# Normalising each 512-query block of a head inside the attention loop instead of after it

## The reference

```
q, k = l2norm(q) * qs, l2norm(k) * ksc;  q, k = rotary_xpos(q, k)
sim  = einsum('bhwid,bhwjd->bhwij', q * 8, k)
mask = (i < j) | (i > j + 512) | (j == -1)
attn = softmax(where(mask, -big, sim))
o    = einsum('bhwij,bhwjd->bhwid', attn, v)
x    = x + o @ wo
```

## Time and profile before

| what | value |
|---|---|
| median of 11 runs | 3704.29 us (3684.22 to 3756.74) |
| time of the profiled execution | 3687.03 us |
| span of its slowest core (core 1) | 3685.5 us |
| busy share of the span, core 1 | PE 70%, PEld 26%, DVE 42%, ACT 15%, POOL 14% |

### The profile page before, as it was taken

How to read it: one execution, slowest core, us unless ns; L and a number is a source line. 1 busy time by engine, 2 the same in 40 slices (tenths; PEclk the granted TensorE clock), 3 DMA queues, 4 the chain that set the end, 5 groups by cost and what they waited for, 6 DMA issues and landing times.

```text
span 3685.5 us, 34257 instructions; the slowest of 8 cores (3657.7 to 3685.5 us)
## 1 busy us (share of the span) xinstructions
PE 2584.8 (70%) x10044; PEld 950.2 (26%) x10044; DVE 1536.2 (42%) x2354; ACT 563.7 (15%) x862; POOL 516.8 (14%) x933
## 2 busy tenths in 40 slices
PE   3636994666787864489999756677777438998970
PEld 2212331221121211034434322112121203343420
DVE  3863664564434334322321256544443422232216
ACT  0100121112121210211011011122212021001101
POOL 3000001000000003052343100000000124235210
PEclk9767997775555558599999877555555859999985
DMA  5022002000000003485575100000000166558522
GB/s 78 0 35 35 15 15 57 1 1 1 1 1 1 1 12 40 67 108 83 69 107 76 32 16 0 1 1 1 0 1 1 21 98 87 82 77 114 77 54 91
DMA packets 136866, 143.08 MB, mean 39 GB/s; under 512 B 33436, under 2 KB 115356, under 8 KB 136688
## 3 DMA queue, kind: packets, MB, share of 16 engines
q0 software_dynamic: 129632, 128.01, 24.0%
q1 hardware_dynamic: 7056, 12.88, 1.0%
HBM read 249.90 MB, written 12.58 MB: 71 GB/s over the span
## 4 chain that ended last, share of the span: by engine, by line
PE 52%; DVE 23%; issue 8%; DMA 7%; ACT 5%; POOL 3%; DVEq 1%; ACTq 0%; SPq 0%; POOLq 0%
PE pA L1074 6%; PE pG L1079 6%; PE pP L292 5%; PE pX3a L1130 5%; PE pX3b L1130 4%; PE pAV L724 4%; DMA W1g<-w_i 3%; DVE g2f L313 3%; DVE scr L679 3%; PE pST L744 2%; PE pST L741 2%; PE pWo L827 2%; PE pS L744 1%; PE pS L741 1%; PE pS L666 1%
## 5 line engine op out<-in xcount | busy, mean ns | idle before, releaser
L1074 PE MATMUL pA<-HN,W1a 128*128 128x512 bf16 (+1 forms) x1408 | 348.7, 392 | 76.2 <-DMA W1g<-w_i 45.2
L1098 DVE SCALAR_TENSOR_TENSOR HG<-pA,b1ac,scr 128x512 bf16<-128x512 f32 (+1 forms) x176 | 132.1, 750 | 553.2 <-ACT scr L1093 553.2
L1079 PE MATMUL pG<-HN,W1g 128*128 128x512 bf16 (+1 forms) x1408 | 341.1, 386 | 0.0
L1056 POOL DMA_DIRECT2D W1a<-w_i x352 | 214.4, 609 | 704.8 <-PE pG L1079 700.3
L1093 ACT ACTIVATE scr<-pG,b1gc 128x512 bf16<-128x512 f32 (+1 forms) x176 | 121.2, 689 | 829.9 <-PE pG L1079 829.9
L527 PE MATMUL pQKV<-AQ,XT 128*128 128x512 bf16 x768 | 228.2, 468 | 8.7 <-DVE rope L501 8.6
L764 DVE TENSOR_TENSOR APT<-APT,m 128x128 bf16<-128x128 bf16 x256 | 57.6, 225 | 418.5 <-ACT APT L760 418.5
L1060 POOL DMA_DIRECT2D W1g<-w_i x352 | 217.5, 618 | 17.2 <-issue 17.2
L810 POOL DMA_DIRECT2D AO<-wo_i x8 | 4.3, 557 | 1484.2 <-DVE AoT L793 1484.2
L1074 PEld LDWEIGHTS pA<-HN,W1a 128*128 128x128 bf16 (+1 forms) x1408 | 138.2, 100 | 258.2 <-issue 107.1
L292 PE MATMUL pP<-WqkvT,XT 128*128 128x512 bf16 x768 | 189.7, 392 | 0.0
(11 more groups left out here) (223 smaller groups left out, 3352.9 us busy)
## 6 DMA issues: line engine op xcount, KB each, us to landing
W1a<-w_i POOLq DMA_DIRECT2D x320, 128.0 KB, 6.4
W1g<-w_i POOLq DMA_DIRECT2D x320, 128.0 KB, 6.7
W2i<-w_i POOLq DMA_DIRECT2D x42, 256.0 KB, 26.6
wst<-Wqkv POOLq DMA_DIRECT2D x24, 256.0 KB, 4.3
AQ<-wqkv_i POOLq DMA_DIRECT2D x16, 384.0 KB, 14.1
XS<-x POOLq DMA_DIRECT2D x16, 256.0 KB, 16.2
x1h<-XS SPq DMA_DIRECT2D x16, 256.0 KB, 2.0
out<-of_sb SPq DMA_DIRECT2D x8, 512.0 KB, 3.1
```

The source lines that it names most:

```text
L1056: E("ge", lambda e, j=j, b5=b5, wa=wa, l=l, bb=bb: e.dma_start(out=W1a[bb][:, 512 * j:512 * j + wa], in_=self.dw1[l, 128 * j:128 * (j + 1) ...
L1074: ins = e.matmul(pA[pp][0:wh, :], W1a[bb][:, 512 * j + 128 * i5:512 * j + 128 * i5 + wh], HNc[:, 512 * j:512 * (j + 1)], start=(j == 0), s ...
L1079: ins = e.matmul(pG[pp][0:wh, :], W1g[bb][:, 512 * j + 128 * i5:512 * j + 128 * i5 + wh], HNc[:, 512 * j:512 * (j + 1)], start=(j == 0), s ...
L1098: E("ve", lambda e, wh=wh, pc=pcglob, pp=pp: e.scalar_tensor_tensor(HG[0:wh, 512 * pc:512 * (pc + 1)], pA[pp][0:wh, :], b1ac[0:wh, pc:pc + ...
```

## The change

The tail of a head is cut into four blocks of 512 queries, each in two halves. `emit_rblock_a(b)` puts the logarithm and the exponential of block b's 512 sums on ScalarE's queue and the copy of block b on VectorE's; `emit_rblock_b(b)` puts the spreading matmul on TensorE's queue and the multiply on VectorE's. For blocks 0, 1 and 2 they are called inside the loop of pass 2: the first half in iteration kc = 4b + 4 after the AV of chunk 4b + 3, the second half in iteration kc = 4b + 5 after the AV of chunk 4b + 4. Block 3 follows after the loop. The waits are on the AV that completes the block, on the block's own exponential and on the block's own matmul. No DMA is changed.

```diff
+            def emit_rblock_a(b):
+                pe_cl = pe_av_last[(h, min(4 * b + 3, NT - 1))]
+                E("se", lambda e, b=b: e.activation(
+                    rw5[0:1, 512 * b:512 * (b + 1)],
+                    pAV[64:65, 512 * b:512 * (b + 1)], AF.Ln),
+                  wait=[("pe", pe_cl)])
+                E("se", lambda e, b=b: e.activation(
+                    rwb[0:1, 512 * b:512 * (b + 1)],
+                    rw5[0:1, 512 * b:512 * (b + 1)], AF.Exp, scale=-1.0))
+                se_rb[b] = C["se"]
+                E("ve", lambda e, b=b, g=g, base=base: e.tensor_copy(
+                    AoT[base:base + 64, 2048 * g + 512 * b:2048 * g + 512 * (b + 1)],
+                    pAV[0:64, 512 * b:512 * (b + 1)]),
+                  wait=[("pe", pe_cl)])
+
+            def emit_rblock_b(b):
+                E("pe", lambda e, b=b: e.matmul(
+                    pAV[64:128, 512 * b:512 * (b + 1)], self.cones[0:1, 0:64],
+                    rwb[0:1, 512 * b:512 * (b + 1)], start=True, stop=True),
+                  wait=[("se", se_rb[b])], inc=[("pe", 1)])
+                pe_rbc[b] = C["pe"]
+                E("ve", lambda e, b=b, g=g, base=base: e.tensor_tensor(
...
+                    pAV[64:128, 512 * b:512 * (b + 1)], op=OP.mult),
+                  wait=[("pe", pe_rbc[b])])
...
                     emit_av(kc - 1, min(640, T - 128 * (kc - 1)))
+                    if (kc - 1) % 4 == 3:
+                        emit_rblock_a((kc - 1) // 4)
+                    if kc >= 5 and (kc - 5) % 4 == 0:
+                        emit_rblock_b((kc - 5) // 4)
             emit_av(NT - 1, min(640, T - 128 * (NT - 1)))
-            E("se", lambda e: e.activation(rw5[:], pAV[64:65, 0:2048], AF.Ln),
-              wait=[("pe", pe_av_done), ("pe", C["pe"])])
-            E("se", lambda e: e.activation(rwb[:], rw5[:], AF.Exp, scale=-1.0))
...
-            for qc in range(4):
-                E("ve", lambda e, qc=qc, g=g, base=base: e.tensor_copy(
...
-                  wait=[("pe", pe_av_done)])
-                E("pe", lambda e, qc=qc: e.matmul(
...
-                  wait=[("se", se_r)], inc=[("pe", 1)])
...
-                E("ve", lambda e, qc=qc, g=g, base=base: e.tensor_tensor(
...
-                  wait=[("pe", pe_rbc[qc])])
+            emit_rblock_a(3)
+            emit_rblock_b(3)
```

More of the change, by code:

```diff
@@ L731, in emit_av @@
                 pe_av_last[(h, kc)] = C["pe"]
+            se_rb = {}
+            pe_rbc = {}
+            def emit_rblock_a(b):
[19 more added lines that the diff above has]
+                E("ve", lambda e, b=b, g=g, base=base: e.tensor_tensor(
+                    AoT[base:base + 64, 2048 * g + 512 * b:2048 * g + 512 * (b + 1)],
+                    AoT[base:base + 64, 2048 * g + 512 * b:2048 * g + 512 * (b + 1)],
+                    pAV[64:128, 512 * b:512 * (b + 1)], op=OP.mult),
+                  wait=[("pe", pe_rbc[b])])
             for kc in range(NT):
@@ L774, in layer_att @@
                     emit_av(kc - 1, min(640, T - 128 * (kc - 1)))
+                    if (kc - 1) % 4 == 3:
+                        emit_rblock_a((kc - 1) // 4)
+                    if kc >= 5 and (kc - 5) % 4 == 0:
+                        emit_rblock_b((kc - 5) // 4)
             emit_av(NT - 1, min(640, T - 128 * (NT - 1)))
-            pe_av_done = C["pe"]
-            E("se", lambda e: e.activation(rw5[:], pAV[64:65, 0:2048], AF.Ln),
-              wait=[("pe", pe_av_done), ("pe", C["pe"])])
-            E("se", lambda e: e.activation(rwb[:], rw5[:], AF.Exp, scale=-1.0))
-            se_r = C["se"]
-            pe_rbc = {}
-            for qc in range(4):
-                E("ve", lambda e, qc=qc, g=g, base=base: e.tensor_copy(
-                    AoT[base:base + 64, 2048 * g + 512 * qc:2048 * g + 512 * (qc + 1)],
-                    pAV[0:64, 512 * qc:512 * (qc + 1)]),
-                  wait=[("pe", pe_av_done)])
-                E("pe", lambda e, qc=qc: e.matmul(
-                    pAV[64:128, 512 * qc:512 * (qc + 1)], self.cones[0:1, 0:64],
-                    rwb[0:1, 512 * qc:512 * (qc + 1)], start=True, stop=True),
-                  wait=[("se", se_r)], inc=[("pe", 1)])
-                pe_rbc[qc] = C["pe"]
-                E("ve", lambda e, qc=qc, g=g, base=base: e.tensor_tensor(
-                    AoT[base:base + 64, 2048 * g + 512 * qc:2048 * g + 512 * (qc + 1)],
-                    AoT[base:base + 64, 2048 * g + 512 * qc:2048 * g + 512 * (qc + 1)],
-                    pAV[64:128, 512 * qc:512 * (qc + 1)], op=OP.mult),
-                  wait=[("pe", pe_rbc[qc])])
+            emit_rblock_a(3)
+            emit_rblock_b(3)
             ve_oT[h] = C["ve"]
```

## The result

The changed kernel takes 3612.71 us (median of 13 runs, 3588.95 to 3713.48), the kernel before 3697.87 (median of 48 runs, 3681.24 to 3816.07). The ratio is 0.9752, interval 0.9722 to 0.9781, which leaves out executions in which the cores of one die ran at a lower granted clock than the others. Of 3697.87 us that is 91.7 us, with about 11 to either side; 88.5 were forecast.

A forecast was written before the change was run, and what follows sets the result against it. TensorE sets the pace in pass 2 and waits for the tail after it. 7.29 - 0.96 - 0.80 = 5.53 us a head, 88.5 for 16 heads, takes the median from 3704.3 to 3616 us; range 3594 to 3636.

The forecast's parts named there:

- The tail: Behind the loop only block 3 stays: 3.03 us to the next head's reduction instead of 10.32, saving 7.29 a head.
- Blocks 0 and 1: In the loop of pass 2, each adds its spreading matmul's time to TensorE: 2 x 0.48 = 0.96 us a head.
- The wait: Spreading matmul of blocks 0 and 1, behind AV: reciprocals come in time, with 0.32 us to spare.
- The size of the matmul: Spreading matmul in the loop: 0.48 us of TensorE's time, between 0.45 and 0.54.
- Block 2: On short chunks 12 and 13: TensorE stalls 0.3 us, then runs 0.48; costs 0.80 a head, bounds 0.45 and 1.3.
- VectorE's and ScalarE's work at nothing: Blocks 0 and 1 in the loop: these engines' work costs nothing, covered by TensorE's own work.
- Stalls in the loop: Rival: each in-loop block makes TensorE wait for its reciprocals; only 20 us gained, 3684 us; chance 7 in 100.
- Table reloads: Rival: ScalarE loads its function table twice per block, 1.283 us each; 66 us slower, 3770; chance 3 in 100.
- A higher clock: Rival: TensorE granted 2.4 instead of 1.2 GHz in pass 2; 200 us more gained, about 3415; chance 2 in 100.
- the lower end of the gain: Whole kernel: bounds of block 2 and of the matmul give a gain of 80 to 95 us, 3609 to 3624.

The follow-up runs named there:

- e7: The changed kernel with all four blocks cut but kept behind the loop, every block waiting for the last AV; a head's period 59.78 us.
- e4_double_ln: The changed kernel with ScalarE's logarithm of blocks 0, 1 and 2 done twice in a row; a head's period 58.86 us against 57.46.
- e5_double_spread: The changed kernel with TensorE's spreading matmul of blocks 0, 1 and 2 done twice in a row; a head's period 58.77 us against 57.46.

## Why the prediction was right, and where its terms were off

**Where the gain comes from.** The forecast was 88.5 us from heads that are 5.53 us shorter; they are 5.56 shorter, and the span lost 90.1. The experiments split the 5.56 step by step:

| step | period, us | saves, us |
|---|---|---|
| before | 63.02 | |
| cut into four blocks, copies ahead of the multiplies, all waiting for the last AV (e7) | 59.78 | 3.24 |
| each block waits for its own AV (e1) | 58.91 | 0.87 |
| blocks 0 to 2 in the loop, second half one chunk later (the change) | 57.46 | 1.45 |
| the same without the one chunk (e2) | 62.59 | -3.68 against e1 |

My theory (A in e1_split_only) was that the loop's cover is what pays. It fell in this form: 4.11 of 5.56 us are there without the loop, as VectorE's copies and multiplies and ScalarE's two passes overlap behind it. The first step changes two things at once. The old tail has three of its four copies among the multiplies, after the exponential; e7 has all four ahead of them, while ScalarE still works. An estimate from the earlier trace rows: that order alone, without any cut, would take three copies with their gaps, 3 x 0.79 = 2.37 us, off the old tail. So most of the 3.24 us may be the order and not the cut; no run tried the order by itself. What the prediction had right is the condition under which the loop adds to it. The prediction's sum did not notice this, because it compared only the whole old tail with the whole new one.

**The tail.** Forecast 3.03 us, measured 3.02. The logarithm took 0.590 instead of the 0.598 of its neighbour in the earlier trace rows, the exponential 0.628 instead of 0.630.

**Blocks 0 and 1.** The wait was right: no idle time, 0.32 us to spare, and e4_double_ln measured that spare by using it up. The size of the matmul was off: 0.56 us instead of 0.48, and above the upper bound of 0.54. I put it between a matmul that follows its like (0.45) and p2's pairs (0.54), because it loads 64 columns and not 128. The step that failed is that reading. The 0.45 is a mean over unlike steps: the first three of the four matmuls of the earlier trace rows follow each other after 0.40, 0.43 and 0.43 us, and from the last to the next head's score matmul (1046.01) it is 0.56. Its row in the kernel before:

```profile
1045.45 0.63 PE L788 MATMUL pAV<-rwb,k_cones 1*64 1x512 bf16 x1
```

So the size was in the trace, at the one of the four that stands before other work, as each does in the loop. What makes the difference is not the change of weights as such. In an earlier stage of the changed kernel (L527), at a granted clock of 0.50, matmuls of 512 columns that load other weights each time, always 128 rows of 128 columns, follow each other after 0.43 us, and each load starts while the matmul before its own runs:

```profile
642.31 0.15 PEld L527 LDWEIGHTS pQKV<-AQ,XT 128*128 128x128 bf16 x1 [0.28 <-issue]
642.74 0.15 PEld L527 LDWEIGHTS pQKV<-AQ,XT 128*128 128x128 bf16 x1 [0.28 <-issue]
```

The 0.53 to 0.57 us stand where the next matmul loads another number of rows: 64, 1 and 128 in turn in p2, the spreading matmul and AV. The trace of core 1 of the changed kernel, run once more, has 2931 pairs of matmuls at 0.50 with no idle time between the two. With the same number of rows the second's load starts within 0.06 us of the first matmul's start in 1482 of 1514 pairs; with another number, in 2 of 1417. No run varied the number of rows by itself.

**Block 2.** The forecast was 0.80, a stall of 0.3 and 0.48 for the matmul. The spreading matmul starts 1.67 us behind p2 of chunk 13 (1084.14 to 1085.81), where the next p2 stood at 1.43 (1035.56 to 1036.99). So it is 0.24 late, as the reciprocals come 0.06 sooner than I had put them; its row shows 0.18 of this as idle time, because the record of AV(12) reaches 0.06 further than the 1.43. With 0.53 for the matmul the next p2 is late by 0.77, 2.20 us behind p2 of chunk 13 (1084.14 to 1086.34). Of these, 0.11 come back by the last logarithm, and 0.66 stay. The prediction let the rest of the loop be late by all of it. So the loop costs 1.12 + 0.66 = 1.78 us where 1.76 was forecast: two errors of opposite sign cancel, and the sum is better than its terms.

**VectorE's and ScalarE's work at nothing.** Right: a second copy in three blocks adds 0.06 us in all, and exp(5) starts at 1009.75, 0.09 behind the new exponential, and AV(5), at 1012.19, has no idle time before it. The cover is not wide: the second copy fills it.

**The rivals.** Stalls in the loop: the mechanism is real, and e2_no_defer shows it, at 2.37 us a block where I had worked out 2.01; the change avoids it by the one chunk between the halves. Table reloads: none; 64 logarithms and 64 exponentials mix with the others under one load for each layer. The Trainium skill (ScalarE: Activation LUTs, "Table sets: the hidden batching unit") lists a set with both functions; the trace agrees with it. A higher clock: the grant is 0.50 before and after, and in the stretch above TensorE is now busy for 84% (375.32 of 444.62), where it was 77% (370.25 of 482.43, from 876.07 to 1358.50 before). The Trainium skill (TensorE: Matmul & The Clock Gate, "Part 1: The HAM clock gate") has sustained work raise the clock. The 0.50 differs from that, and the measurement decides; no run here shows what would raise it in this stage.

**Slips in the working.** After the first multiply VectorE has six more instructions in the old tail, not seven; the 10.32 us do not rest on the count. By the prediction's own terms the reloads cost eight loads and 1.12 us a head, so they decide from 0.77 us for a load on, not 0.67. And with the matmul at 0.54 together with block 2 at 1.3 the lower end of the gain is 79 us, not 80. None of the three moves the forecast.

## What to carry to other kernels

When a chain over three engines stands behind a loop, see first what can be had in its place: blocks, the copies ahead of the multiplies, and each piece waiting for its own producer only gave 4.11 of 5.56 us a head there. Whether the order of the copies would have given most of that by itself is open. Moved into the loop, a piece pays only if the engine that sets the pace finds its input ready: put the second half as many steps later as the first half takes, and check the spare time by the reader's own queue (here 0.32 us with one chunk between, and a loss of 3.68 us a head against e1_split_only without it). A matmul that is moved between others is to be priced by a row in which it stands before the same kind of work (here 0.56 us to the next head's score matmul), not by the mean of a series of its like (0.45).

## What the runs showed of the hardware

- At the granted clock of 0.50 a matmul of 512 columns took 0.43 us to the next where both load the same number of rows, also with other weights (L527), and 0.53 to 0.57 where the next loads another number of rows: its load then starts directly before it, and not during the matmul before (1017.24 against 1016.25 to 1016.43 in e5_double_spread).
- On 512 columns ScalarE took 0.590 us for a logarithm from `pAV` in one partition, 0.598 for an exponential from `pST` in 128, and 0.628 for one from `rw` in one. In these rows the longer time goes with the source and not with the number of partitions; no run varied the source alone.
- A wait on a semaphore that has already reached its value cost nothing that the trace shows: in e1_split_only the logarithm follows the last exponential within 0.09 us (1030.16 + 0.28 to 1030.53).
